# Layer 0 of a four-layer graph kernel: the copies of the upper and the lower parts of Q and K leave in separate groups, each with its own semaphore

## What is computed

```python
q = (x @ Wq.T + bq).reshape(B, N, H, Dh).transpose(0, 2, 1, 3)
k = (x @ Wk.T + bk).reshape(B, N, H, Dh).transpose(0, 2, 1, 3)
v = (x @ Wv.T + bv).reshape(B, N, H, Dh).transpose(0, 2, 1, 3)
...
scores = jnp.einsum('bhnd,bhjcd->bhnjc', q, kc) / jnp.sqrt(jnp.asarray(Dh, dtype=q.dtype))
scores = jnp.clip(scores, -10.0, 10.0)
...
attn = jax.nn.softmax(scores, axis=-1)
ctx = jnp.einsum('bhnjc,bhjcd->bhnd', attn, vc)
```

## Time and profile before

| | us |
|---|---|
| median of 3 runs | 2105.55 |
| the profiled execution | 2097.68 |
| its span in the trace | 2095.8 |
| busy: PE, DVE, ACT, POOL | 1662.8, 1600.5, 1339.4, 124.7 |
| granted TensorE clock, mean over the span | 0.905 |

### The profile page before, as it was taken

The page is one execution under the profiler, slowest core; times in us unless marked ns, Lnnn a source line. Parts: engine busy times, 40 slices in busy tenths (PEclk is TensorE's granted clock), DMA queues, the critical chain, the costliest instruction groups (busy, mean ns, idle before and its releaser), DMA issues. The chain is left out here.

```text
span 2095.8 us, 36839 instructions
## 1 busy us (share of the span) xinstructions
PE 1662.8 (79%) x13620; PEld 1056.3 (50%) x13620; DVE 1600.5 (76%) x2710; ACT 1339.4 (64%) x1751; POOL 124.7 (6%) x130
## 2 busy tenths in 40 slices
PE   2888877888778657799998976777877657999997
PEld 1333333433334336677776765556655553455544
DVE  3676867878778855788888999898898856766674
ACT  2665645656556448676677798898888834455453
POOL 0000100101100010000000000000000000000000
PEclk7988989899999859899999988889998879999999
DMA  7545263352533231111111111122211211000000
GB/s 208 131 101 122 64 145 86 93 134 69 134 93 102 69 114 42 41 42 44 48 41 52 41 68 66 62 63 72 70 64 62 71 56 40 11 11 20 10 11 20
DMA packets 74923, 146.51 MB, mean 70 GB/s; under 512 B 11937, under 2 KB 34722, under 8 KB 74754
## 3 DMA queue, kind: packets, MB, share of 16 engines
q1 hardware_dynamic: 74754, 144.23, 24.4%
HBM read 101.85 MB, written 8.78 MB: 53 GB/s over the span
## 5 line engine op out<-in xcount | busy, mean ns | idle before, releaser
L1068 ACT ACTIVATE g<-s_all,steep_d 128x1024 fp8e4<-128x1024 f32 x608 | 642.4, 1136 | 39.6 <-DMA s_all<-s_rows 18.4
L1003 PE MATMUL acc<-parts,g 128*128 128x102 bf16 (+1 forms) x6144 | 414.1, 228 | 29.3 <-DVE sums L1159 21.7
L1003 PEld LDWEIGHTS acc<-parts,g 128*128 128x128 fp8e4 x6144 | 398.2, 99 | 62.3 <-issue 45.6
L985 PE MATMUL post<-parts,edge 128*128 128x396 bf16 (+1 forms) x1024 | 232.4, 383 | 86.4 <-DVE base L1167 86.4
L561 ACT ACTIVATE e<-s_ps 128x1024 f32<-128x1024 f32 x256 | 248.6, 1023 | 24.8 <-PE s_ps L420 18.3
L1152 DVE TENSOR_TENSOR g<-g,edge 128x1024 int32<-128x1024 int32 x192 | 228.0, 1219 | 34.6 <-ACT g L1068 34.6
L706 DVE SCALAR_TENSOR_TENSOR e<-e,bound 128x1024 f32<-128x1024 f32 x160 | 188.8, 1214 | 34.6 <-ACT e L561 33.5
L416 PE MATMUL s_ps<-qs,ks 128*128 128x512 f32 x512 | 200.6, 503 | 9.9 <-issue 8.0
L432 PE MATMUL sum_ps<-e,pick 128*32 128x256 f32 x2048 | 144.5, 402 | 71.7 <-DVE e L703 42.5
L985 PEld LDWEIGHTS post<-parts,edge 128*128 128x128 fp8e4 x1024 | 101.8, 102 | 193.4 <-issue 107.9
L567 ACT ACTIVATE chunk<-ctx_ps 128x512 f32<-128x512 f32 x128 | 76.4, 597 | 178.6 <-PE ctx_ps L441 178.6
(11 more groups left out here) (158 smaller groups left out, 2117.1 us busy)
## 6 DMA issues: line engine op xcount, KB each, us to landing
s_all<-s_rows SPq DMA_DIRECT2D x96, 512.0 KB, 3.6
inv_all<-inv_rows SPq DMA_DIRECT2D x256, 128.0 KB, 2.9
qs<-split SPq DMA_DIRECT2D x128, 128.0 KB, 3.1
ks<-split SPq DMA_DIRECT2D x128, 128.0 KB, 2.4
x<-in_x SPq DMA_DIRECT2D x8, 512.0 KB, 6.8
inv_rows<-inv SPq DMA_DIRECT2D x32, 128.0 KB, 1.7
adj_in<-in_adj SPq DMA_DIRECT2D x8, 512.0 KB, 4.3
out_x<-x SPq DMA_DIRECT2D x8, 512.0 KB, 3.2
```

The lines of the kernel that those rows point to most:

```text
L985: ins = pe.matmul(self.post[:, it % 2, 0:H * 3 * W1].rearrange("p (h k c) -> p h k c", h=H, k=3), self.c.edge[:, jt, it * P:(it + 1) * P], ...
L1003: ins = pe.matmul(self.acc[:, bank, o:o + self.NS], self.g[:, h % RING, jt, it * P:(it + 1) * P], self.upper[par][:, jt, h, :, :].rearrang ...
L1068: act.activation(self.g[:, h % RING, jt, :], self.s_all[:, h % 2, :], ACT.Relu, bias=self.steep_d[par][:, jt, h:h + 1], scale=STEEP, satur ...
```

## The change

`stack` now takes one part of `split` and the two copies that are made of it, and a semaphore of its own, so that Q's 16 copies become a group of 8 from part 0 and a group of 8 from part 1, and K's likewise. A group of part 0 waits for `high` (`q_hi`, `k_hi`) and a group of part 1 for `low` (`q_split`, `k_split`). `high` of K waits for Q's group of part 0 alone, and `low` of K has a wait that it did not have, for Q's group of part 1 (`q_lo_stacked`); `high` and `low` of the next Q wait in the same way for K's groups. PE waits for all four. No computing instruction changes or moves, and there are 32 copies as before; within K the order of the copies is now part 0 twice (rows 0 and 64), then part 1 twice.

```diff
-    STACK = 16 * COPIES * H
+    STACK = 16 * (COPIES // 2) * H
...
-            def stack(n, par, dst, parts, split_done, stacked):
-                sp.wait_ge(split_done, n + 1)
-                for copy in range(COPIES):
+            def stack(n, dst, part, copies, computed, stacked):
+                sp.wait_ge(computed, n + 1)
+                for copy in copies:
                     for h in range(H):
-                        sp.dma_start(dst[par][copy * DH:(copy + 1) * DH, h, :].bitcast(F32),
-                                     split[h * DH:(h + 1) * DH, parts[copy], :].bitcast(F32)).then_inc(stacked, 16)
-
-            def stack_q(n, par):
-                stack(n, par, qs, (0, 0, 1, 1), q_split, q_stacked)
-
-            def stack_k(n, par):
-                stack(n, par, ks, (0, 1, 0, 1), k_split, k_stacked)
+                        sp.dma_start(dst[copy * DH:(copy + 1) * DH, h, :].bitcast(F32),
+                                     split[h * DH:(h + 1) * DH, part, :].bitcast(F32)).then_inc(stacked, 16)
+
+            def stack_q_hi(n, par):
+                stack(n, qs[par], 0, (0, 1), q_hi, q_hi_stacked)
+
+            def stack_q_lo(n, par):
+                stack(n, qs[par], 1, (2, 3), q_split, q_lo_stacked)
+
+            def stack_k_hi(n, par):
+                stack(n, ks[par], 0, (0, 2), k_hi, k_hi_stacked)
+
+            def stack_k_lo(n, par):
+                stack(n, ks[par], 1, (1, 3), k_split, k_lo_stacked)
...
             def k(n):
-                high(n, k_projected, bk, k_hi, q_stacked, STACK * (n + 1))
+                high(n, k_projected, bk, k_hi, q_hi_stacked, STACK * (n + 1))
...
-            def low(n, hi_done, bias, done):
+            def low(n, hi_done, bias, done, free):
                 dve.wait_ge(hi_done, n + 1)
+                dve.wait_ge(free, STACK * (n + 1))
...
-                            low(n, k_hi, bk, k_split)
+                            low(n, k_hi, bk, k_split, q_lo_stacked)
```

More of the change, by code:

```diff
@@ L240, in layer0 @@
         nm = Norm(c, 0, aux)
-        q_projected, q_hi, q_split, q_stacked = (c.sem(f"q_{k}") for k in ("projected", "hi", "split", "stacked"))
-        k_projected, k_hi, k_split, k_stacked = (c.sem(f"k_{k}") for k in ("projected", "hi", "split", "stacked"))
+        q_projected, q_hi, q_split, q_hi_stacked, q_lo_stacked = (
+            c.sem(f"q_{k}") for k in ("projected", "hi", "split", "hi_stacked", "lo_stacked"))
+        k_projected, k_hi, k_split, k_hi_stacked, k_lo_stacked = (
+            c.sem(f"k_{k}") for k in ("projected", "hi", "split", "hi_stacked", "lo_stacked"))
         v_projected, v_ready, late_ready = c.sem("v_projected"), c.sem("v_ready"), c.sem("late_ready")
@@ L283, in _ @@
             load_x(1, x_loaded[1])
-            def stack(n, par, dst, parts, split_done, stacked):
-                sp.wait_ge(split_done, n + 1)
-                for copy in range(COPIES):
+            def stack(n, dst, part, copies, computed, stacked):
+                sp.wait_ge(computed, n + 1)
+                for copy in copies:
                     for h in range(H):
-                        sp.dma_start(dst[par][copy * DH:(copy + 1) * DH, h, :].bitcast(F32),
-                                     split[h * DH:(h + 1) * DH, parts[copy], :].bitcast(F32)).then_inc(stacked, 16)
-            def stack_q(n, par):
-                stack(n, par, qs, (0, 0, 1, 1), q_split, q_stacked)
-            def stack_k(n, par):
-                stack(n, par, ks, (0, 1, 0, 1), k_split, k_stacked)
+                        sp.dma_start(dst[copy * DH:(copy + 1) * DH, h, :].bitcast(F32),
[8 more added lines that the diff above has]
+                stack(n, ks[par], 1, (1, 3), k_split, k_lo_stacked)
             def prepare(n, par):
-                stack_q(n, par)
-                stack_k(n, par)
+                stack_q_hi(n, par)
+                stack_q_lo(n, par)
+                stack_k_hi(n, par)
+                stack_k_lo(n, par)
             def inverses(b, half, group):
@@ L329, in stage @@
                     wait_apart(c, sp, s_ready, 32 * b + 64)
-                    stack_q(b + 1, 1 - par)
-                    stack_k(b + 1, 1 - par)
+                    stack_q_hi(b + 1, 1 - par)
+                    stack_q_lo(b + 1, 1 - par)
+                    stack_k_hi(b + 1, 1 - par)
+                    stack_k_lo(b + 1, 1 - par)
                 inverses(b, 1, 0)
@@ L458, in stacks @@
             def stacks(n):
-                pe.wait_ge(q_stacked, STACK * (n + 1))
-                pe.wait_ge(k_stacked, STACK * (n + 2))
+                pe.wait_ge(q_hi_stacked, STACK * (n + 1))
+                pe.wait_ge(q_lo_stacked, STACK * (n + 1))
+                pe.wait_ge(k_hi_stacked, STACK * (n + 2))
+                pe.wait_ge(k_lo_stacked, STACK * (n + 2))
             def stage(b, par, first, more):
@@ L510, in _ @@
             act.sem_inc(chunk_copied, 1)
-            act.sem_inc(k_stacked, STACK)
+            act.sem_inc(k_hi_stacked, STACK)
+            act.sem_inc(k_lo_stacked, STACK)
             act.wait_ge(loaded, 80)
@@ L525, in q @@
             def q(n):
-                high(n, q_projected, bq, q_hi, k_stacked, STACK * (n + 1))
+                high(n, q_projected, bq, q_hi, k_hi_stacked, STACK * (n + 1))
             def k(n):
-                high(n, k_projected, bk, k_hi, q_stacked, STACK * (n + 1))
+                high(n, k_projected, bk, k_hi, q_hi_stacked, STACK * (n + 1))
             def v_out(n, par):
@@ L687, in prepare @@
                 dve.tensor_scalar(minus[:, :], c.ident[:, :], NEG, None, ALU.mult)
-                low(n, q_hi, bq, q_split)
-                low(n, k_hi, bk, k_split)
+                low(n, q_hi, bq, q_split, k_lo_stacked)
+                low(n, k_hi, bk, k_split, q_lo_stacked)
                 bounds(0)
```

## The result

The changed kernel takes 2066.55 us in the median of four runs (2063.89 to 2069.89), the kernel before 2105.24 (2094.33 to 2108.16). The ratio is 0.9838, with a 95% interval of 0.9807 to 0.987: 27 to 41 us less. The forecast was 2073.8, 31.8 us less. In the trace the last update of x in layer 0 starts at 706.50 us instead of 742.55: 36.05 us sooner.

A forecast was written before the change was run, and what follows sets the result against it. Two chains, SP's copies and DVE's work from Q's last copy, meet at step 15's weighing, SP's the later. Stage 0 4.4, stages 1 to 6 18.8, start 4.0, clock 4.6: 31.8 us off 2105.6 gives 2073.8, range 2061 to 2087.

The forecast's parts named there:

- SP's pause: SP's idle gap between issuing Q's and K's copies, 5.34 us in stage 2, 4.41 in stage 0, goes entirely.
- C: Rival: the DMA engines need the pause, so only the start gains, 2.4 us: 2103; chance 0.06.
- D: Rival: K's copies directly behind delay Q's last group by 5 us, so lower K starts later: +9, 2115; chance 0.05.
- DVE starts 1.15 us earlier: Before lower K, DVE waits for Q's last copy instead of ACT: 1.15 us per stage, 6.9 in six.
- The wait at step 15: DVE's wait for `inv_all` before that weighing goes in stages 1 to 6, 11.9 us; 3 to 4 stay in stage 0.
- The gain there is not passed on: DVE's idling before step 14's clip brings nothing: step 13's sums follow DVE at once, then PE sets the residual.
- Stage 0: Its gain is SP's whole pause, 4.41 us, since 6.67 of wait plus 1.15 is more.
- The start: In the program's start ACT's table load for the exponentials is free at 47.4 instead of 51.49; taken as 4.0 us.
- The clock: PE's sums behind step 15 mostly keep 2.4 GHz: about 0.9 us in five of six stages, 4.6 us.
- rival B: PE's spread-out steps 11 to 13 lose clock, some 1.1 us per stage; gain only 20.6 us, 2085; chance 0.22.

The follow-up runs named there:

- e1: The changed kernel, but SP issues a stack's 16 copies only when both parts are written; ratio 0.9938 to the kernel before.
- e2: The changed kernel, but ACT waits for all 16 copies of Q before it writes upper K; ratio 0.9921 to the kernel before.
- e7: The changed kernel, with SP issuing the store `inv_rows` four copies before the end of K's second group; ratio 0.9842 to the kernel before.
- e8: The changed kernel, with SP issuing Q's two groups ahead of pair 3's four `inv_all` copies; ratio 0.9802 to the kernel before.
- e9: The changed kernel with the copy orders of e7 and e8 together; median 2051.22 us, ratio 0.9787 to the kernel before.

## Why the prediction was right, step by step

- **SP's pause.** Right: 0.04 to 0.05 us in all seven stages. Q's first group alone releases ACT, which starts 7.68 us behind Q's first copy in stage 2 (8.0 predicted), and the copies directly behind did not delay Q's second group: lower K starts at + 12.75 us where it started at + 14.11. Rivals C and D are out.
- **DVE starts 1.15 us earlier.** Right: from Q's first copy to lower K the sum over stages 1 to 6 fell from 84.14 to 77.23 us, 6.9 as predicted.
- **The wait at step 15** (11.9 us in stages 1 to 6). Gone, as predicted, and 4.6 us are left in stage 0 (3 to 4).
- **"The gain there is not passed on".** This is the step that failed, a term put at nothing. Lower K to step 15 took 18.21 us in the mean before, without the wait, and 17.56 after: 3.9 us in six stages. It was read off stage 2, where the sums of step 13 follow DVE at once and the stretch lost only 0.4 us; in stage 1 it lost 1.4. There PE was late before:

```profile
196.41 2.95 PE L165 MATMUL aux<-wv,h_t 128*128 128x128 f32 x16
199.29 1.07 PE L432 MATMUL sum_ps<-e,pick 128*32 128x256 f32 x16
```

  V's projection started 4.24 us behind lower K, since ACT's late start had held up two products and the scores before it, at the lower clock; the sums of step 12 came 7.12 us behind lower K. Now V's projection starts 1.34 us behind lower K, in all seven stages, and those sums 4.15 to 5.06 us. e1, which has ACT's early release, has the short chain (17.53); e2, which has not, the long one (18.21). Stages 1 to 6 together gave 22.7 us and not 18.8.
- **Stage 0:** 5.05 us, not 4.4: K's copies took 10.12 us there instead of 11.56.
- **The start:** 3.5 us at ACT's table load, 4.1 at the first copy of stage 0; 4.0 predicted.
- **The clock:** 4.6 us predicted in five of six stages. The inversion behind step 15 came 4.61 us behind it in the mean of seven stages, and 3.98 now: 4.4 us. That the sum fits is in part luck: 0.9 of it came in stage 0, where nothing was counted, and stages 1 to 6 gave 3.6. In stages 1 and 3 the sums still ran at 1.93 us, after pauses of 1.85 and 1.94 us, and in stage 2 after 1.94 us at 1.07. The pause right before the sums does not decide it alone. In stage 2 PE's work of steps 11 to 13 is spread now, with pauses of 2.51 and 1.70 us, and runs at the lower clock, 0.50 granted from 262 to 268 us against 1.00 from 251 to 257. V's projection takes 3.67 us there where it took 2.07 (3.5 to 3.8 in the stages 2, 4 and 6, 2.05 in the others):

```profile
251.00:257.00 6.00, 6.00 (x48) 2.37 (x40) 5.94 (x6) 2.54 (x3) 0.00 (x0) 1.00 0.96 219
262.00:268.00 6.00, 4.30 (x16) 3.15 (x15) 3.98 (x4) 2.72 (x4) 0.00 (x0) 0.50 0.88 190
```

  The Trainium skill (TensorE: Matmul & The Clock Gate, Part 1) states that activity is what releases the clock; the trace agrees, and it bears out that half of rival B. Its price did not come, since DVE, not PE, sets the pace from the sums of step 12 on: lower K to step 15 takes 17.44 us in stage 1, with V's projection at 2.05, and 17.54 in stage 2, with 3.67. Only stage 4 (17.89) may have paid 0.4.

The stretches up to step 15 gave 27.8 us, those behind it 4.2, the start 4.1: 36.05. The profiled span shrank by 32.2 us only; from layer 0's end to the end of the span it is 1353.3 us before and 1357.1 after, and 1353.6 to 1359.0 in the other twelve traces, whose code is the same there. So one execution's scatter covers it, though the kernel before has the lowest value of all fourteen. The 38.7 us between the medians lie within the interval of 27 to 41, and so does the forecast's 31.8.

## What to carry to other kernels

A queue that waits in order is a chain of its own: look where it stands still, and what is queued behind that gap, even if it serves quite another step. Where two chains meet, the gain is that of the shorter cut plus the wait, and a later cut of one alone brings little until the other is cut too (in one trace each, e7 and e8 brought 4 us, e9 15). Read the slack of a chain as the time from the landing of its last copy to the instruction that uses it, in each stage, and not off the gain of another change: a gain up to the meeting point can be lost behind it, as in e8. And read a stretch in several stages: from lower K to step 15 the change saved 0.4 us in stage 2 and 1.4 in stage 1.

## What was not expected of the hardware

In the kernel before, the same 16 copies of 128 KB took 10.03 to 11.56 us to issue, and from the store `inv_rows` to the first of its loads 1.9 to 4.1 us passed. Copies issued directly behind a group did not hold it up: the last copy of Q in stages 0 to 6 landed 1.8 to 2.8 us after its issue before and 1.8 to 2.7 in the changed kernel, where K's follow at once. In the changed kernel, after pauses of TensorE of 1.94 us the sums ran at either level (1.07 or 1.93 us), so that the length of the last pause alone does not decide the clock; what else does was not tried.
